# Setup of a post-norm layer kernel: row sums of chunks 0 and 1 as products straight from the squares, clip logarithms of two chunks on GpSimd, the output weight's maxima ahead of one weight split

## The reference, cut to what matters

```python
r = jax.nn.sigmoid(jnp.einsum('btd,ed->bte', x, Wr))
k = jnp.einsum('btd,ed->bte', x, Wk)
v = jnp.einsum('btd,ed->bte', x, Wv)
dec = jax.nn.sigmoid(decay)
log_decay = jnp.log(jnp.clip(dec, 1e-07))
scale = jnp.exp(t * log_decay[None, :])
kv = k * v
cum = jnp.cumsum(kv / jnp.clip(scale, 1e-10)[None], axis=1)
state = cum * scale[None]
y = _rmsnorm(r * state, ln_w)          # y * rsqrt(mean(y*y) + 1e-6) * w
x = _layernorm(x + jnp.einsum('btd,ed->bte', y, Wo), axis=-1)
...
h = jax.nn.gelu(jnp.einsum('bsd,hd->bsh', x, bw1) + b1, approximate=False)
x = _layernorm(x + jnp.einsum('bsh,dh->bsd', h, bw2) + b2, axis=-1)
```

## Time and profile before

| | us |
|---|---|
| median of 3 runs | 821.07 (820.94 to 821.75) |
| the profiled execution, its own time | 821.11 |
| its span in the trace | 819.3 |
| PE busy | 798.8 (97%) |
| DVE busy | 771.3 (94%) |
| ACT busy | 679.9 (83%) |
| POOL busy | 295.3 (36%) |

### The profile page before, as it was taken

One profiled execution on the slowest core, in us unless ns is written; L12 is line 12 of the kernel. 1 busy time (PEld: TensorE's weight loads), 2 busy tenths in 40 slices (PEclk: granted clock), 3 DMA queues, 4 the chain that ended last, 5 costly groups with the idle time before them and its releaser, 6 DMA issues.

```text
span 819.3 us, 16575 instructions
## 1 busy us (share of the span) xinstructions
PE 798.8 (97%) x5174; PEld 505.7 (62%) x5174; DVE 771.3 (94%) x1472; ACT 679.9 (83%) x973; POOL 295.3 (36%) x572
## 2 busy tenths in 40 slices
PE   6989999999999999999999999999999999999986
PEld 4555666656666656666656666655666665666654
DVE  7998999999999999999999999999999999999887
ACT  7987888888888888888888888888888888887775
POOL 3343323344223344333344333344333334332344
PEclk9999999999999999999999999999999999999999
DMA  8513553434553434553434454444454344444313
GB/s 261 99 27 78 129 125 84 110 94 102 128 128 86 115 81 105 125 128 92 113 79 109 118 128 100 105 89 106 112 128 105 100 97 104 106 102 104 78 26 104
DMA packets 168286, 86.27 MB, mean 105 GB/s; under 512 B 128572, under 2 KB 163912, under 8 KB 168264
## 3 DMA queue, kind: packets, MB, share of 16 engines
q1 hardware_dynamic: 147288, 52.97, 27.5%
q0 software_dynamic: 4608, 16.78, 10.4%
q10 hardware_dynamic: 16368, 16.25, 5.6%
HBM read 20.45 MB, written 16.78 MB: 45 GB/s over the span
## 4 chain that ended last, share of the span: by engine, by line
PE 88%; DVE 4%; POOL 2%; ACT 2%; issue 2%; DMA 0%; SPq 0%; POOLq 0%; DVEq 0%; ACTq 0%
PE ps_r L375 28%; PE ps_o L496 26%; PE ps_f L446 19%; PE ps_r L446 6%; PE ps_o L401 6%; PE ps_o L406 3%; DVE hid_lo L1008 1%; DVE u L959 1%; ACT hid L678 1%; DVE u_st L967 0%; PE ps_s L383 0%; DMA x_in<-in_L_attn_x_dram 0%; POOL root L1322 0%; POOL y_sqs L1310 0%; DVE state L923 0%
## 5 line engine op out<-in xcount | busy, mean ns | idle before, releaser
L496 PE MATMUL ps_o<-w2T,hid_hi 128*128 128x256 f16 x992 | 218.9, 273 | 3.4 <-DVE hid_lo L1008 3.0
L496 PE MATMUL ps_o<-w2T,hid_lo 128*128 128x256 f16 x992 | 218.8, 272 | 0.0
L375 PE MATMUL ps_r<-x_t,proj_hi 128*128 128x512 f16 x768 | 197.1, 379 | 1.2 <-issue 0.7
L446 PE MATMUL ps_f<-x_t,w1T 128*128 128x512 f16 x768 | 181.7, 379 | 1.6 <-DVE x_t L992 1.3
L678 ACT ACTIVATE hid<-ps_f,rows_c,f_scale 128x512 f32<-128x512 f32 x192 | 145.2, 774 | 42.2 <-PE ps_f L446 37.1
L1008 DVE SCALAR_TENSOR_TENSOR hid_lo<-hid,hid_scale,hid_hi 128x1024 f16<-128x1024 f32 (+1 forms) x136 | 160.3, 1222 | 0.9 <-POOL hid_hi L1343 0.6
L1310 POOL TENSOR_TENSOR y_sqs<-y_sq 128x512 f32<-128x512 f32 x32 | 46.7, 1459 | 309.6 <-ACT y_sq L653 309.6
L375 PEld LDWEIGHTS ps_r<-x_t,proj_hi 128*128 128x128 f16 x768 | 74.7, 98 | 91.3 <-issue 2.8
L713 ACT ACTIVATE hid_hi<-hid,hid_scale 128x2048 f16<-128x2048 f32 (+2 forms) x72 | 127.9, 1778 | 3.2
L446 PEld LDWEIGHTS ps_f<-x_t,w1T 128*128 128x128 f16 x768 | 74.9, 98 | 79.7 <-issue 1.6
L375 PE MATMUL ps_r<-x_t,proj_lo 128*128 128x512 f16 x384 | 114.2, 379 | 0.2 <-DVE proj_lo L1084 0.2
(11 more groups left out here) (191 smaller groups left out, 1332.2 us busy)
## 6 DMA issues: line engine op xcount, KB each, us to landing
x_in<-in_L_attn_x_dram SPq DMA_DIRECT2D x32, 512.0 KB, 4.1
res<-b_row POOLq DMA_DIRECT2D x32, 512.0 KB, 4.5
out_dram<-res ACTq DMA_DIRECT2D x31, 512.0 KB, 2.9
w_in<-in_L_ffn_w_dram SPq DMA_DIRECT2D x2, 1024.0 KB, 8.8
x_t<-x_st SPq DMA_TRANSPOSE x59, 3.7
b_row<-in_L_ffn_b_dram SPq DMA_DIRECT2D x1, 512.0 KB, 12.7
proj_in<-in_L_attn_Wk_dram SPq DMA_DIRECT2D x1, 256.0 KB, 3.8
proj_in<-in_L_attn_Wv_dram SPq DMA_DIRECT2D x1, 256.0 KB, 4.1
```

The lines of the kernel that those rows point to most:

```text
L375: last = nc.tensor.matmul(ps_r[:, m, :], w[:, m, dc, ec * P:(ec + 1) * P], xx[:, :, dc, :], start=(n == 0), stop=(n == 3 * DC - 1))
L446: last = nc.tensor.matmul(f1_bank[hc % NF], w1T[:, hc, dc, :], xx[:, :, dc, :], start=(dc == 0 and n == 0), stop=(dc == DC - 1 and n == 1))
L496: last = nc.tensor.matmul(o_tok[:, tt, :], hh[:, hc, tt * P:(tt + 1) * P], w2T[:, :, hc, :], start=(hc == 0 and n == 0), stop=(hc == HC - ...
```

## The change

It touches the setup alone; the loop's text is the same but for the counts of three waits, because chunks 0 and 1 no longer pass through `ysqs`, `block_sums` and `sum_rows`.

```diff
@@ TensorE
+            def sum_squares(c):
+                pe.wait_ge(s_yq, c + 1)
+                pe.wait_ge(s_xtmp, c + 3)
+                for tt in range(TT):
+                    for dc in range(DC):
+                        last = nc.tensor.matmul(ps_sums[:, tt:tt + 1], y_sq[:, dc, tt * P:(tt + 1) * P],
+                                                ones_col[:, :], start=(dc == 0), stop=(dc == DC - 1))
+                last.then_inc(s_sums, 1)
             def O(c, k, last_chunk=False):
                 pe.wait_ge(s_yq, c + 1)
-                if k < 2:
-                    sum_rows(c)
+                if k == 1:
+                    sum_squares(c)
@@ TensorE, prologue
                 TX(2, 0, 2, True, slot=2)
+                sum_squares(0)
                 R(1, False, looped=False, ecs=(1,), slot=1)
@@ ScalarE, clip_table: Exp with the bias for all four chunks; clip_excess is gone
@@ ScalarE, prologue
                 xsq(1, 0, 1)
-                clip_excess(2)
                 r_gates(0, 0, (0,))
                 clip_table(2)
                 xh(1, 1, slot=1)
                 signs(w1_in, w1_sgn, s_w1_in, s_sgn)
+                r_gates(0, 0, (1,))
                 xsq(2, 0, 2)
-                r_gates(0, 0, (1,))
                 wo_split_hi()
@@
                 r_gates(1, 1, (0,))
-                clip_excess(3)
                 yh(0)
@@
-                act.wait_ge(s_ysqs, 1)
+                act.wait_ge(s_sums, 1)
                 ysq(1, (0,), y=y_second)
@@ VectorE
+            def mean_first(c):
+                dve.wait_ge(s_sums, c + 1)
+                nc.vector.tensor_scalar(ms[:, :], ps_sums[:, 0:TT], 1.0 / D, 4.0 * EPS_RMS, ALU.mult,
+                                        ALU.add).then_inc(s_ms, 1)
@@ VectorE, prologue: wo_maxima() from behind take_xbound(1, 1) to ahead of proj_split_lo(2);
-                block_sums(0)
+                mean_first(0)
                 yl(0)
                 xl(2, 2, slot=2)
-                mean_sq(0)
@@
-                block_sums(1)
                 yl(1, y_second)
-                mean_sq(1)
+                mean_first(1)
@@ GpSimd: neg_log is gone; for chunks 2 and 3
+                for dc in range(DC):
+                    nc.gpsimd.tensor_scalar(clip_g[:, dc, part], steps[:, part], dec_c[:, 1, dc:dc + 1], -LOG_CLIP,
+                                            ALU.mult, ALU.min).then_inc(s_clip_late, 1)
+            clip_logs_late(2)        # ahead of unscales(0, 0)
                 unscales(1, 1)
-                ysqs(0)
+                clip_logs_late(3)
@@
-                ysqs(1)
```

More of the change, by code:

```diff
@@ L101, in postln_layer_kernel @@
         log_clip = sb("log_clip", [P, 1])
-        neg_log_clip = sb("neg_log_clip", [P, 1])
-        neg_log = sb("neg_log", [P, DC])
         w_max = sb("w_max", [P, 6])
@@ L197, in postln_layer_kernel @@
         s_winv, s_wscl, s_proj_hi, s_alpha = sem("winv_s"), sem("wscl_s"), sem("proj_hi_s"), sem("alpha_s")
-        s_clip, s_exp, s_nlog, s_excess = sem("clip_s"), sem("exp_s"), sem("neg_log_s"), sem("clip_excess_s")
+        s_clip, s_exp, s_clip_late = sem("clip_s"), sem("exp_s"), sem("clip_late_s")
         s_lnw, s_wo_hi = sem("lnw_s"), sem("wo_hi_s")
@@ L380, in sum_rows @@
             def sum_rows(c):
-                pe.wait_ge(s_ypart, c + 1)
+                pe.wait_ge(s_ypart, c - 1)
                 nc.tensor.matmul(ps_sums, fold[:, :, :].rearrange("p q t -> p (q t)"),
@@ L727, in proj_split_hi @@
                                      scale=w_scl[:, n:n + 1]).then_inc(s_proj_hi, 1)
[L729 to L735, removed]
             def clip_table(n):
@@ L741, in clip_table @@
                 else:
-                    act.wait_ge(s_excess, DC * n - DC)
+                    act.wait_ge(s_clip_late, DC * n - DC)
                 for dc in range(DC):
                     part = clip_g[:, dc, n * CH:(n + 1) * CH]
[L745 to L748, removed]
+                    nc.scalar.activation(part, part, ACT.Exp, bias=log_clip[:, :]).then_inc(s_exp, 1)
             def wo_split_hi():
@@ L936, in block_sums @@
             def block_sums(c):
-                dve.wait_ge(s_ysqs, c + 1)
+                dve.wait_ge(s_ysqs, c - 1)
                 nc.vector.tensor_reduce(y_part[:, :, :].rearrange("p tt q -> p (tt q)"),
@@ L947, in mean_sq @@
                                                op1=ALU.mult).then_inc(s_msall, 1)
-                dve.wait_ge(s_msall, c + 1)
+                dve.wait_ge(s_msall, c - 1)
                 nc.vector.tensor_reduce(ms[:, :], ms_all[:, :, :], AX.X, ALU.add).then_inc(s_ms, 1)
+            def mean_first(c):
+                dve.wait_ge(s_sums, c + 1)
+                nc.vector.tensor_scalar(ms[:, :], ps_sums[:, 0:TT], 1.0 / D, 4.0 * EPS_RMS, ALU.mult,
+                                        ALU.add).then_inc(s_ms, 1)
             def residual1(c, j, src=o_tok, first=False):
@@ L1127, in _ @@
             nc.vector.tensor_scalar_mul(w_inv[:, 2:3], w_inv[:, 2:3], 0.5).then_inc(s_winv, 1)
-            proj_split_lo(2)
             def wo_maxima():
@@ L1136, in wo_maxima @@
                                         apply_absolute_value=True).then_inc(s_wmax, 1)
+            wo_maxima()
+            proj_split_lo(2)
             def wo_scale():
@@ L1179, in prologue @@
                 take_xbound(1, 1)
-                wo_maxima()
                 scans(0, 0, 0)
@@ L1388, in _ @@
             nc.gpsimd.memset(log_clip[:, :], LOG_CLIP)
-            nc.gpsimd.memset(neg_log_clip[:, :], -LOG_CLIP)
             nc.gpsimd.iota(steps[:, :], [[1, T]], base=0, channel_multiplier=0,
@@ L1399, in _, with clip_logs_late @@
             nc.gpsimd.tensor_copy(fold[:, 1:TT, :], fold[:, 0:1, :].to_broadcast([P, TT - 1, P // TT]))
-            pool.wait_ge(s_setup_a, 2)
-            nc.gpsimd.tensor_scalar(neg_log[:, :], dec_c[:, 1, :], -1.0, 1.0, ALU.mult, ALU.mult).then_inc(s_nlog, 1)
+            def clip_logs_late(n):
+                pool.wait_ge(s_setup_a, 2)
+                part = slice(n * CH, (n + 1) * CH)
+                for dc in range(DC):
+                    nc.gpsimd.tensor_scalar(clip_g[:, dc, part], steps[:, part], dec_c[:, 1, dc:dc + 1], -LOG_CLIP,
+                                            ALU.mult, ALU.min).then_inc(s_clip_late, 1)
+            clip_logs_late(2)
             pool.wait_ge(s_winv, 1)
```

## The result

| | before | after |
|---|---|---|
| median of the runs, us | 821.07 (820.94 to 821.75, 6) | 824.50 (823.39 to 824.88, 6) |
| ratio | | 1.0039, 95% interval 1.0026 to 1.0051 |
| span of the profiled execution | 819.3 | 822.8 |

A forecast was written before the change was run, and what follows sets the result against it. Bound: TensorE's unbroken chain from 63.14 us, the end of F2(0)'s last wait, set by VectorE's dense stretch. An earlier start, less two row sums of 1.7 us partly filling waits, left it 0.15 to 0.2 later: 821.3, range 820.1 to 822.2.

The forecast's parts named there:

- the prediction's sum: VectorE's dense stretch before the loop starts and ends 0.15 to 0.2 us later, so 821.11 becomes 821.3.
- That nothing of the loop is changed: Premise: the change is worth only what it moves the end of F2(0)'s last wait, at 63.14 us.
- step 2: Setup, clip_excess off ScalarE: scan at about 17.3, work up to the second y 0.5 us sooner, sum_bounds(0) at 25.8, not 26.30.
- Wo's maxima are free: Setup: the maxima fit VectorE's idle 0.86 us ahead of 14.93, cost nothing, and TensorE gains 0.3.
- steps 4 to 8: TensorE from sum_bounds(0): each sum_squares 1.7 us, R(1, ecs=(1,)) 0.8 late, F1(0) at 45.75, O(1) 0.9 late, residual1(1) 0.15 late.
- GpSimd's logarithms cost nothing but for the port: Setup: GpSimd takes logarithms of 2 x 1.37 us, priced by decay_f, where it idles; price nothing but for the port.
- The one-column product at 0.11 a record: TensorE: weight loads pace sum_squares at 0.11 us per record, 16 records, 1.7 us each.
- the one on GpSimd blocking VectorE: Rival: before 26 us a GpSimd pair starting just ahead of a scan or y delays VectorE up to 0.7; 822.0, chance 0.10.
- a loss would need a new wait in a loop with unchanged text: Argument against the rival that the loop behind 63 us falls into another rhythm; that rival's chance 0.07.

The follow-up runs named there:

- e10: Changed kernel with only padding added, so that x_st, x_t, the results, x1_st and x1_t start at multiples of 256 bytes; 822.63 us (ratio 1.0019).
- e15: Changed kernel, tiles on 256, chunk 1's bound taken before kvg of chunk 0, xh(1) ahead of clip_table(2), both row sums new; 821.76 us.
- e17: e15 with two tiny VectorE instructions added at about 4.5 us, where VectorE waits for its input; 821.31 us (ratio 1.0002).
- e3: Changed kernel, tiles in their old places, row sums of chunks 0 and 1 back to the old way; 821.57 us (ratio 1.0007).
- e13: Changed kernel on 256 with old row sums; VectorE takes chunk 1's bound between k_sb and kvg of chunk 0, so the scale precedes the scan; 820.92 us.
- e14: e13 with ScalarE making xh(1) ahead of clip_table(2); 820.84 us (ratio 0.9994).
- e6: Kernel before, tiles in place, with only Wo's maxima sooner and ScalarE's one exchange of order; 821.10 us.
- e11: e3 with one more wait: VectorE's first scan waits until GpSimd has the scale of chunk 1; 821.17 us.
- e2: Kernel before with the two small tiles declared last, so every tile from w_max on lies 64 bytes lower; 821.80 us (ratio 1.0008).
- e1: Changed kernel with the two deleted small tiles still declared, so later tiles stand where they stood before; 822.69 us (ratio 1.0021).
- e4: Changed kernel, tiles in their old places, clip_excess (late logarithms) back on ScalarE, row sums new; 822.22 us (ratio 1.0013).
- e8: Kernel before with Wo's maxima sooner, ScalarE's exchange, and only sum_squares(0) new; 822.63 us (821.75 to 824.27).

## Why the prediction was wrong

The medians close the account: after 824.50; tiles on 256 (e10) 822.63; the scale ahead of the scan (e15) 821.76; two instructions (e17) 821.31; before 821.12. So 1.87 is the place of the tiles, 0.87 the two moves that bring `xh(1)` forward (with the old row sums the freed scale alone gave 0.65, e3 less e13, and `xh(1)` ahead of the table 0.08 more), 0.45 the end, and 0.2 is left, the net that the prediction's sum has. That sum sets a gain of 0.5 against the row sums; measured apart they are 0.3 (before less e14, within the scatter) and 0.5 (e17 less e14).

Two steps failed. **That nothing of the loop is changed**, so that the change is worth what it moves the end of `F2(0)`'s last wait: the loop's text is the same, but its tiles lie 64 bytes lower, and two waits for loads cost 2.19 in the profiled execution and 1.87 by the medians. And **the 0.5 of step 2**, below. Either alone puts the kernel above 822.2 (e10 at 822.63; 824.50 less 0.87 is 823.6), so both had to be seen for the range to hold.

1. *Wo's maxima are free*: right (17.79 in place of 18.07 in the changed kernel; e6).
2. *The scan starts 0.6 sooner, and everything up to the second y 0.5*: **failed**. The first half held (17.44), the second didn't: -0.5 became +0.28, and the 0.8 between them went through steps 4 to 8 almost undiminished to 64.01, where 63.3 was forecast. The step followed ScalarE and VectorE and left out GpSimd, which makes the scale for `xh(1)` just there. (e13, with the scale free, has the 0.50.)
3. *GpSimd's logarithms cost nothing but for the port*: nearly right in time (e11), wrong in price. `clip_g` takes 2.04 each [4.08 for two], not 1.37 for two as `decay_f`, and slows VectorE's own pair beside it from 0.87 to 1.11. There was room for it.
4. to 8.: right. In the changed kernel every distance from `sum_bounds(0)` to `F2(0)`'s wait is within 0.1 of the forecast. With `sum_bounds(0)` at 25.73 and the tiles on 256, e15 and e17 land at 821.76 and 821.31. The one-column product at 0.11 a record was right to 0.01; the Trainium skill, TensorE: Matmul & The Clock Gate, section LDWEIGHTS, has 107 ns, and the trace 106.

Of the rivals, the one on GpSimd blocking VectorE, by the port that they share, named the wrong victim. The prediction had the row in which a GpSimd element is held up until a scan ends, took it as an argument *against* a loss ("in the row it is GpSimd that waits"), and didn't ask who waits for GpSimd. The Trainium skill, SBUF — State Buffer, section Who interferes with whom, calls the shared port pair an exclusive lock for whoever comes first; here the scan at 17.44 and the scale at 17.43 start together, the scan takes its usual 1.22, and the scale ends 0.37 behind it. The trace agrees that one of them waits; which one comes first it can't tell at 0.01. And "a loss would need a new wait in a loop with unchanged text" (0.07) was taken for a reason against, where it is what happened: the loop's text was unchanged, its addresses weren't. The diff of the two kernels shows the two deleted declarations. The 0.37 at the end was in no rival; nothing in the trace of the kernel before announces it.

## What to carry to other kernels

Making one instruction start sooner moves it beside others: list what the other engines do at its new time, who shares a port with it, and who waits for those. A declaration added or removed moves every tile behind it; print the addresses of the tiles that DMA transposes read and write before and after, and keep them at a multiple of 256 bytes. A load's median time to landing doesn't tell whether it holds anybody up: look at the slowest ones, and at what else is in flight then. Before a change of some tenths of a microsecond is judged, take out such effects of place, or they are read as the change's own.

## What the runs showed of the hardware

- Transposing loads between tiles that start at a multiple of 256 bytes move 290 GB/s and land after 3.6 to 3.7 us; 32 or 64 bytes off it is 212 GB/s and 4.3.
- A packet of 16 KB of the `instruction` queue takes 0.9 to 2.0 us, 1.0 in the median of all traces. The last two packets of a load start only when it is through (66.76 to 67.64 in the changed kernel, 139.42 to 140.38 in e2), and the load lands 1.6 to 1.7 late.
- A GpSimd operation of one element per partition beside a VectorE scan of 1.22 us takes 1.60, not 0.56; a 128x512 `tensor_scalar` of multiply and minimum takes GpSimd 2.04 us, where multiply and add took 0.69.
- A wait of 0.5 of VectorE for itself comes and goes with two instructions 800 us earlier (e15, e17).
- Behind `sum_squares(0)` the granted TensorE clock fell to 0.50 of full speed (1.2 of 2.4 GHz) in the profiled executions of e1, e4 and e10 (5 of their 33 have a mean clock of 0.995, not 0.997 to 0.999, and lie some 1.5 us above the others). The stretches of one in e10, the clock third from the right:

```profile
28.00:30.00 2.00, 2.00 (x16) 1.62 (x16) 1.96 (x2) 2.00 (x2) 1.90 (x3) 0.92 0.02 4
30.00:32.00 2.00, 2.00 (x6) 0.76 (x5) 1.97 (x5) 1.98 (x4) 1.82 (x3) 0.50 0.00 0
32.00:34.00 2.00, 2.00 (x9) 0.71 (x7) 1.90 (x4) 0.86 (x2) 1.09 (x2) 0.72 0.00 0
```

  TensorE was busy all the time, with 1.7 us of one-column fp32 products just ahead. The changed kernel has the same products at the same place and showed it in none of 6 executions, e8 in none of 11, e15 and e17, 0.9 sooner, in none of 22; why isn't settled.
